# Handing the row maxima of an attention step to the score banks through memory instead of through TensorE

## The chip, the cores and the metric

The kernel runs on one core of one Trainium2 chip. The metric is the device time of one execution in microseconds (us). All times below are either such whole times or come from one profiled execution of the kernel before the change.

## What is computed

Two transformer-like layers with a residual stream of 4 x 1024 tokens of 128 values. The change touches only the attention of layer 0:

```
qkv = X @ W_qkv                      # 16 heads of 64, batch 4, 1024 tokens
scores = einsum("bqhd,bkhd->bhqk", q, k) / scale
weights = softmax(scores)            # over the keys
attn = einsum("bhqk,bkhd->bqhd", weights, v)
s = attn @ W_out
x = x + s * silu(mixture_of_experts(xn))
```

The rest (the router and the experts of layer 0, a recurrence and a 4-bit feed-forward part in layer 1) runs before and behind it and is not changed.

## The kernel before, in words

`layer0_attention` handles N = 32 pairs of heads (4 batches x 8 pairs), in a hardware loop whose body is two pairs. A pair `n` has 16 steps `t`. Steps 0 to 7 are the first half of the queries (512 of them), steps 8 to 15 the second; each step is one tile of 128 keys against 512 queries for both heads, so a score tile is 128 x 1024. Two steps make a visit `p = t // 2`; `VISIT[p]` lists small extra items that TensorE does in that visit: projections `K0`, `K1`, `Q0`, `Q1` of a later pair, `V0`, `V1`, the denominators `den0`, `den1`, the output projections `out0`, `out1`. All items write one bank, `ps_x`, so an item waits until the item before it in the list has been read (`bank_free`).

The softmax needs a bound of each query's scores before the exponential. That bound is the row maximum over a cheaper score product: in every step `row_max` on TensorE writes the tile `ps_m` (queries as rows, one bank pair, so it waits for the reduction of the one before: semaphore `m_done`), and VectorE reduces it into `mxh`. Eight of these make a unit (one half of the queries of one pair), and then one small reduction collects them. Units run `EARLY` steps ahead of the scores that need them.

Scores are accumulated on top of the negated maximum. There are two score banks, `ps_s[0]` and `ps_s[1]`, used by even and odd steps. Before TensorE may accumulate (`scores`, six matmuls, waits for `seeded`), the bank must hold the negated maximum, the same in all 128 rows. In the kernel before this is done in four stages: TensorE transposes the maxima with the identity (items `max0` and `max1`, L1241, into `ps_x`); VectorE multiplies them with a mask into `shift` (L1560); TensorE multiplies `shift` with ones into `ps_s[0]` (`spread`, L1293, once before each half, waits for the exponential that last read the bank); ScalarE copies that bank to a tile in SBUF, `shift_all` (`keep_shift`, L1444), and from there into the banks of the other seven steps (`seed`, L1449).

ScalarE then takes the exponential from the score bank into a ring of 8 probability tiles (L1464), GpSimd adds these up for the denominators (L1529), TensorE multiplies them with V three steps late (`values`, L1301). SyncE moves V, the batch's normalised inputs and a part of the experts' weights between memory and SBUF; it issues its DMAs from one queue in program order, and each wait there holds back all that stand behind it. The order of work on every engine is written out by hand in the loop bodies.

## Time and profile before

| what | before |
|---|---|
| median of 3 runs (lowest to highest) | 1915.51 us (1915.51 to 1917.42) |
| the profiled execution's own time | 1918.03 us |
| its span in the trace | 1916.2 us |
| mean granted TensorE clock | 0.982 of full speed |

The attention loop fills about three quarters of the span. Because its body repeats, one pair read closely in the middle of the run tells what all 32 cost; times are read as start and duration within the span.

### The profile page before, as it was taken

How to read it: one execution, taken by the hardware profiler on the slowest of the kernel's cores; microseconds unless marked ns; L12 is line 12 of the kernel's file. 1: busy time of each engine (PE TensorE's matmuls, PEld its weight loads, DVE VectorE, ACT ScalarE, POOL GpSimd, SP SyncE). 2: the span in 40 equal slices, each digit the busy share in tenths (PEclk: the TensorE clock that was granted, in tenths of full speed). 3: DMA queues.
4: the chain of work that ended last, by engine and by line, in shares of the span. 5: the costliest groups of instructions: out<-in, count | busy, mean ns of one | idle time of the engine just before them, and what ended most of it. 6: DMA issues, size and time to landing. Idle time of an engine off the chain costs nothing. (4 is left out here: it accounts for less than half of the span.)

```text
span 1916.2 us, 32241 instructions
## 1 busy us (share of the span) xinstructions
PE 1776.4 (93%) x9630; PEld 958.1 (50%) x9630; DVE 1486.4 (78%) x2052; ACT 1485.6 (78%) x2017; POOL 1434.9 (75%) x870
## 2 busy tenths in 40 slices
PE   5799999999999999999999999999999899985688
PEld 4444444444444444444444444444444488863456
DVE  6777777777777777777777777777777698888896
ACT  4488888888888888888888888888888688874553
POOL 4388888888888888888888888888888456765663
PEclk9999999999999999999999999999999999997898
DMA  7101010101011010101010101011010477531000
GB/s 248 46 13 55 11 56 15 59 11 55 22 44 42 25 55 11 55 11 55 12 55 19 55 20 46 22 44 56 11 55 11 153 230 247 158 99 50 1 17 28
DMA packets 98438, 108.95 MB, mean 57 GB/s; under 512 B 8161, under 2 KB 88097, under 8 KB 95202
## 3 DMA queue, kind: packets, MB, share of 16 engines
q1 hardware_dynamic: 93410, 98.26, 16.1%
q0 software_dynamic: 4992, 10.27, 1.6%
q8 instruction: 16, 0.26, 0.1%
q14 instruction: 20, 0.16, 0.0%
HBM read 53.12 MB, written 27.38 MB: 42 GB/s over the span
## 5 line engine op out<-in xcount | busy, mean ns | idle before, releaser
L1529 POOL TENSOR_TENSOR psum_k<-psum_k,probs 128x1024 f32<-128x1024 f32 x384 | 926.4, 2412 | 183.7 <-ACT probs L1464 168.6
L1546 DVE TENSOR_REDUCE mxh<-ps_m 128x2 f32<-128x1024 f32 x518 | 628.4, 1213 | 276.1 <-PE ps_m L1273 275.7
L1464 ACT ACTIVATE probs<-ps_s 128x1024 f32<-128x1024 f32 x512 | 496.4, 1022 | 132.4 <-PE ps_s L1286 93.2
L1301 PE MATMUL ps_v<-probs,V 128*64 128x512 f32 x2056 | 489.8, 597 | 0.0
L1449 ACT ACTIVATE ps_s<-qkv_raw 128x1024 f32<-128x1024 f32 x449 | 445.9, 1030 | 7.1
L1570 DVE RECIPROCAL e_y_row<-e_y_row 128x128 f32<-128x128 f32 x256 | 241.8, 945 | 30.2 <-ACT e_y_row L1420 21.1
L1301 PEld LDWEIGHTS ps_v<-probs,V 128*64 128x64 f32 x2056 | 137.6, 137 | 224.9 <-issue 188.4
L1529 POOL TENSOR_TENSOR psum_k<-probs 128x1024 f32<-128x1024 f32 x64 | 152.4, 2381 | 65.7 <-ACT probs L1464 57.9
L1286 PE MATMUL ps_s<-e_ew 64*128 64x512 f32 x1536 | 198.9, 390 | 1.1 <-ACT qkv_raw L1444 1.0
L1286 PEld LDWEIGHTS ps_s<-e_ew 64*128 64x128 f32 x1536 | 145.9, 184 | 28.6 <-ACT qkv_raw L1444 1.4
L859 POOL DMA_INDIRECT results<-e_y_row,e_y_at x92 | 103.7, 1128 | 67.4 <-ACT e_y_row L800 45.2
L1273 PE MATMUL ps_m<-e_ew 64*128 64x512 f32 x524 | 131.5, 498 | 11.4 <-DVE mxh L1546 10.2
L1273 PE MATMUL ps_m<-k_hi,q_hi 64*128 64x512 f32 x512 | 128.0, 496 | 4.0 <-DVE mxh L1546 3.6
L1273 PEld LDWEIGHTS ps_m<-e_ew 64*128 64x128 f32 x524 | 49.1, 184 | 114.8 <-DVE mxh L1546 68.2
L1286 PE MATMUL ps_s<-q_hi,k_lo 64*128 64x512 f32 x512 | 101.6, 391 | 0.0
L1286 PE MATMUL ps_s<-q_hi,k_hi 64*128 64x512 f32 x512 | 101.5, 391 | 0.0
L1286 PE MATMUL ps_s<-q_lo,k_hi 64*128 64x512 f32 x512 | 101.2, 389 | 0.0
L1273 PEld LDWEIGHTS ps_m<-k_hi,q_hi 64*128 64x128 f32 x512 | 47.6, 183 | 106.5 <-DVE mxh L1546 60.1
L784 ACT ACTIVATE e_relu<-e_ps_z 128x512 f32<-128x512 f32 x124 | 74.2, 598 | 26.5 <-PE e_ps_z L713 25.6
L905 DVE TENSOR_TENSOR e_h_lo<-e_relu,e_h_hi 128x512 fp32r<-128x512 f32 x124 | 87.5, 711 | 1.2 <-ACT e_h_hi L789 1.2
L901 DVE TENSOR_TENSOR e_relu<-e_relu 128x512 f32<-128x512 f32 x108 | 74.5, 690 | 15.5 <-ACT e_relu L784 15.2
L789 ACT ACTIVATE e_h_hi<-e_relu 128x512 fp32r<-128x512 f32 x124 | 78.2, 631 | 6.0 <-DVE e_relu L901 5.9
(322 smaller groups left out, 2938.1 us busy)
## 6 DMA issues: line engine op xcount, KB each, us to landing
e_ew<-w_split SPq DMA_DIRECT2D x23, 1024.0 KB
V<-e_x_raw SPq DMA_DIRECT2D x33, 512.0 KB, 3.6
xs_hi<-xh SPq DMA_DIRECT2D x16, 512.0 KB, 4.1
xs_lo<-xl SPq DMA_DIRECT2D x16, 512.0 KB, 4.7
rows<-in_blank_d SPq DMA_DIRECT2D x4, 1483.5 KB, 16.2
e_x_raw<-rows SPq DMA_DIRECT2D x23, 258.0 KB, 3.0
we_raw<-in_experts_d SPq DMA_DIRECT2D x33, 128.0 KB, 2.5
w_split<-we_hi SPq DMA_DIRECT2D x32, 128.0 KB, 1.9
```

The costliest lines, as they stand in the source:

```text
L789: nc.scalar.activation(h_hi[:, q % NH, :], r2[:, q % NH, :], ACT.Copy).then_inc(hi_done, 1)
L859: nc.gpsimd.indirect_dma_start(g.results[:, :], bass.IndirectOffsetOnAxis(ap=y_at[s][:, t, 0:1], axis=0), y_row[s][:, t, :], None).then_in ...
L901: nc.vector.tensor_tensor(r2[:, q % NH, :], r[:, q % NZ, :], r[:, q % NZ, :], ALU.mult).then_inc(sq_done, 1)
L905: nc.vector.tensor_tensor(h_lo[:, q % NH, :], r2[:, q % NH, :], h_hi[:, q % NH, :].bitcast(F32), ALU.subtract).then_inc(lo_done, 1)
L1273: ins = nc.tensor.matmul(m[:, x, :], q_hi[par][rows, q:q + P], k_hi[par][rows, kh * CH:(kh + 1) * CH], start=True, stop=True)
L1286: ins = nc.tensor.matmul(o[:, x, :], lhs[par][rows, keys], rhs[par][rows, qs], start=False, stop=True, skip_group_check=True)
L1301: ins = nc.tensor.matmul(ps_v[rows, :], V[par][:, kt, rows], probs[:, t % RING, x, :], start=kt == 0, stop=kt == KT - 1)
L1449: nc.scalar.activation(ps_s[t % 2][:, :, :], shift_all[:, :, :], ACT.Copy).then_inc(seeded, 1)
L1464: nc.scalar.activation(probs[:, t % RING, :, :], ps_s[t % 2][:, :, :], ACT.Exp, scale=SCALE).then_inc(p_done, 1)
L1529: nc.gpsimd.tensor_tensor(acc, probs[:, (t - 1) % RING, :, :] if kt == 1 else acc, probs[:, t % RING, :, :], ALU.add).then_inc(add_done, 1)
L1546: nc.vector.tensor_reduce(mxh[:, kh, t, :], max_bank(unit, i)[:, :, :], AX.X, ALU.max).then_inc(m_done, 1)
L1570: ins = nc.vector.reciprocal(rden[:, cols], den[:, cols])
```

## The change

The maxima no longer pass through TensorE and VectorE. The small reduction writes them to `mx` (128 x 2 x 4). SyncE stores them to a buffer of 4 KB in memory, `g.peaks`, in an order that turns them into rows (1024 separate elements of 4 bytes), waits for that transfer, and loads the row broadcast to all 128 partitions of `peak[hf]` (512 KB). ScalarE copies `peak`, times -1, into the score banks in all 16 steps. `EARLY` goes from 3 to 4. The items are spread anew over the visits, with at most one of them between the scores and `values`; `K0` is made one pair earlier, in the last visit; ScalarE reads the first item of a visit before it seeds the banks, and the second one after it.

The constants and the tables of items:

```diff
-    EARLY = 3
+    EARLY = 4
-    VISIT = [("out0", "K0"), ("den1", "Q0"), ("max1", "V0"), ("K1",), ("out1",), ("den0", "Q1"), ("max0", "V1"), ()]
-    LATE = ("K1", "out1")
+    VISIT = [("out0",), ("Q0", "den1"), ("V0",), ("K1",), ("Q1", "den0"), ("V1",), ("out1",), ("K0",)]
-    FIRST = ["K0", "Q0", "K1", "Q1", "V0", "V1", "V2", "max0", "V3"]
+    FIRST = ["K0", "Q0", "K1", "Q1", "V0", "V1", "V2", "V3", "K0+"]
```

On SyncE:

```diff
+            def spread(unit, hf):
+                sp.wait_ge(mx_done, unit + 1)
+                sp.dma_start(g.peaks[hf:hf + 1, :].rearrange("a (x t q) -> q (a x) t", x=2, t=4), mx[:, :, :],
+                             allow_slow_non_contiguous=True).then_inc(mx_out, 16)
+                sp.wait_ge(mx_out, unit * 16 + 16)
+                sp.dma_start(peak[hf][:, :, :].rearrange("p x c -> p (x c)"), g.peaks[hf:hf + 1, :].to_broadcast([P, 2 * CH])).then_inc(peak_in, 16)
...
+                spread(n * 2 + 1, 1)
                 expert_part(n)
                 load_part(n + 1)
+                spread(n * 2 + 2, 0)
+                spread(n * 2 + 3, 1)
                 expert_part(n + 1)
                 load_part((n + 2) % N)
+                spread(n * 2 + 4, 0)
```

On TensorE:

```diff
-            def max_rows(n, name):
-                bank_free(n, name)
-                pe.wait_ge(mx_done, 1 if n is None else n * 2 + (2 if name == "max1" else 3))
-                for x, rows in enumerate(HEADS):
-                    ins = nc.tensor.matmul(bank(n, name)[rows, 0:P], mxw[:, x, :], g.ident[:, :], start=True, stop=True)
-                ins.then_inc(x_ready, 1)
...
-                    if t % KT == KT - 1:
-                        pe.wait_ge(shift_done, n * 2 + t // KT + 2)
-                        pe.wait_ge(p_done, P0 + n * STEPS + t)
-                        spread(1 - t // KT, 0).then_inc(spread_ready, 1)
                     for name in VISIT[p][:1]:
-                        if name not in LATE:
-                            item(n, par, name, b)
+                        item(n, par, name, b)
```

On ScalarE:

```diff
-            def keep_shift(k):
-                act.wait_ge(spread_ready, k)
-                nc.scalar.activation(shift_all[:, :, :], ps_s[0][:, :, :], ACT.Copy).then_inc(seeded, 1)
+            def seed(n, t):
+                hf = t // KT % 2
+                if t % KT < 2:
+                    act.wait_ge(peak_in, peaks_of(n, t))
+                act.wait_ge(p_done, P0 + n * STEPS + t - 1)
+                nc.scalar.activation(ps_s[t % 2][:, :, :], peak[hf][:, :, :], ACT.Copy, scale=-1.0).then_inc(seeded, 1)
...
                     for name in VISIT[p][:1]:
-                        if name[:3] != "den":
-                            read(n, name, 1 - par)
+                        read(n, name, par if name == "K0" else 1 - par)
+                    for k in (t + 1, t + 2):
+                        seed(n, k)
                     if p == 0:
                         keep_values(n * 2 + 1)
+                        expert_part(n)
```

On VectorE one operation goes:

```diff
-            def shifts(n, name):
-                hf = int(name[3])
-                v.wait_ge(x_ready, nth(n, name))
-                nc.vector.tensor_tensor(shift[hf][:, :].rearrange("p (j q) -> p j q", j=4),
-                                        bank(n, name)[:, 0:P].unsqueeze(1).to_broadcast([P, 4, P]),
-                                        mask[:, :].unsqueeze(2).to_broadcast([P, 4, P]), ALU.mult).then_inc(shift_done, 1)
```

On VectorE the order behind the reductions of the 16 steps becomes: `out0` added after 1; `Q0` and the experts' part after 3; parts of the reciprocal after 4, 5, 6 and 8; `K1` after 7; `Q1` and the normalising product after 9; reciprocal after 10, 11, 12 and 14; `out1` added after 13; `K0` and the second normalising product after 15.

Three places of the program show how the instructions move. The first is TensorE in the visit of steps 4 and 5 and the one behind it, before: `ps_m` is the row maximum's tile, `mxw` the collected maxima, `V0` the values of this pair.

```order
L1273 MATMUL ps_m<-k_hi1,q_hi1 128x512 [waits m_done]
L1273 MATMUL ps_m<-k_hi1,q_hi1 128x512
L1201 REGISTER_ALU
L1241 MATMUL ps_x<-ident,mxw 64x128 [waits mx_done,xv_done]
L1241 MATMUL ps_x<-ident,mxw 64x128
L1301 MATMUL ps_v<-probs,V0 64x512 [waits p_done]
...
L1273 MATMUL ps_m<-k_hi1,q_hi1 128x512 [waits m_done]
L1273 MATMUL ps_m<-k_hi1,q_hi1 128x512
L1373 REGISTER_ALU [waits shift_done]
L1293 MATMUL ps_s0<-shift0,ones_r 128x512 [waits p_done]
L1293 MATMUL ps_s0<-shift0,ones_r 128x512
```

The transposition of the maxima stands ahead of the values, and one visit or two later the spreading matmuls stand there, each behind a wait; in the changed kernel neither line exists, and the row maximum is followed by at most one item and then by the values.

The second place is ScalarE behind the exponential of step 7, where the second half of the queries begins. Before:

```order
L1464 ACTIVATE probs<-ps_s1 128x1024 [waits add_done]
L1443 REGISTER_ALU
L1444 ACTIVATE qkv_raw<-ps_s0 128x1024 [waits spread_ready]
L1472 REGISTER_ALU
L1448 REGISTER_ALU [waits seeded]
L1449 ACTIVATE ps_s1<-qkv_raw 128x1024 [waits p_done]
L1410 REGISTER_ALU
L1412 ACTIVATE k_hi1<-ps_x 128x512 [waits x_ready]
```

And in the changed kernel:

```order
L1463 ACTIVATE probs<-ps_s1 128x1024 [waits add_done]
L1408 REGISTER_ALU
L1410 ACTIVATE k_hi1<-ps_x 128x512 [waits x_ready]
L1445 REGISTER_ALU
L1446 REGISTER_ALU [waits peak_in]
L1447 ACTIVATE ps_s0<-peak1 128x1024 [waits p_done]
L1446 REGISTER_ALU [waits peak_in]
L1447 ACTIVATE ps_s1<-peak1 128x1024 [waits p_done]
```

The copy out of the bank has become a copy into it, the count of ScalarE's large instructions is the same (two for these two banks), the reading of the item stands ahead of them, and the wait is now for a DMA.

The third place is SyncE's queue in the first pair of the loop body, where only DMAs and their waits matter. Before:

```order
L1149 DMA V<-e_x_raw 128x8x128 [waits v_ready]
...
L1170 DMA xs_hi<-xh 128x1024
...
L1171 DMA xs_lo<-xl 128x1024
...
L1155 DMA w_split<-we_hi 128x256
```

And in the changed kernel:

```order
L1147 DMA V<-e_x_raw 128x8x128 [waits v_ready]
...
L1177 DMA xs_hi<-xh 128x1024
...
L1178 DMA xs_lo<-xl 128x1024
...
L1163 DMA peaks<-mx 128x8x1 [waits mx_done]
...
L1166 DMA peak<-peaks 128x1024 [waits mx_out]
...
L1153 DMA w_split<-we_hi 128x256
```

The store and the broadcast load stand behind the three large loads of every second pair and ahead of the stores of the experts' part.

## Rows read from the trace of the kernel before

**Rows 1.** The windows view of one pair: length, busy time by engine, granted clock.

```profile
745.97:790.72 44.75, 43.53 (x247) 20.86 (x245) 34.03 (x38) 37.31 (x46) 36.98 (x21) 1.00 0.05 17
```

**Rows 2.** One line's instructions (once per pair): duration, first and last start.

```profile
L1402 ACT ACTIVATE wo<-wout_raw x32: 292/294/298, 121.5 to 1509.5; 128x128 f32 x32
```

**Rows 3.** Timeline of TensorE: start, duration, what, idle time before it.

```profile
755.62 0.50 PE L1273 MATMUL ps_m<-k_hi,q_hi 64*128 64x512 f32 x2
756.30 1.08 PE L1250 MATMUL ps_x<-psum_k,ones 128*64 128x512 f32 x4 [0.17 <-DVE e_ew L1554]
757.20 1.89 PE L1301 MATMUL ps_v<-probs,V 128*64 128x512 f32 x8
...
761.74 0.50 PE L1273 MATMUL ps_m<-e_ew 64*128 64x512 f32 x2
762.56 0.44 PE L1241 MATMUL ps_x<-ident,mxw 128*64 128x128 f32 x4 [0.32 <-DVE e_ew L1554]
762.83 1.89 PE L1301 MATMUL ps_v<-probs,V 128*64 128x512 f32 x8
...
767.37 0.50 PE L1273 MATMUL ps_m<-e_ew 64*128 64x512 f32 x2
767.94 0.49 PE L1293 MATMUL ps_s<-shift,ones_r 64*128 64x512 f32 x2
768.37 1.94 PE L1301 MATMUL ps_v<-probs,V 128*64 128x512 f32 x8
...
771.13 0.50 PE L1273 MATMUL ps_m<-e_ew 64*128 64x512 f32 x2
...
772.95 0.49 PE L1273 MATMUL ps_m<-e_ew 64*128 64x512 f32 x2
773.37 1.94 PE L1301 MATMUL ps_v<-probs,V 128*64 128x512 f32 x8
...
776.10 0.50 PE L1273 MATMUL ps_m<-e_ew 64*128 64x512 f32 x2
...
778.21 0.50 PE L1273 MATMUL ps_m<-e_ew 64*128 64x512 f32 x2 [0.22 <-DVE mxh L1546]
```

**Rows 4.** Timeline of ScalarE over one visit.

```profile
755.12 1.94 ACT L1464 ACTIVATE probs<-ps_s 128x1024 f32<-128x1024 f32 x2 [0.61 <-PE ps_s L1286]
757.42 0.60 ACT L1420 ACTIVATE e_y_row<-ps_x 128x512 f32<-128x512 f32 x1 [0.36 <-PE ps_x L1250]
757.91 1.97 ACT L1449 ACTIVATE ps_s<-qkv_raw 128x1024 f32<-128x1024 f32 x2
```

**Rows 5.** Timeline of VectorE: reduction, collecting, subtraction, reciprocal.

```profile
760.46 1.22 DVE L1546 TENSOR_REDUCE mxh<-ps_m 128x2 f32<-128x1024 f32 x1 [1.46 <-PE ps_m L1273]
761.72 0.17 DVE L1549 TENSOR_REDUCE mxw<-mxh 128x8 f32<-128x16 f32 x1
761.81 0.69 DVE L1554 TENSOR_TENSOR e_ew<-ps_x,e_ew 128x512 fp32r<-128x512 f32 x1
...
764.37 0.95 DVE L1570 RECIPROCAL e_y_row<-e_y_row 128x128 f32<-128x128 f32 x1
```

**Rows 6.** DMA issues: how many, KB each, median us from issue to landing.

```profile
V<-e_x_raw SPq DMA_DIRECT2D x33, 512.0 KB, 3.6
...
xs_lo<-xl SPq DMA_DIRECT2D x16, 512.0 KB, 4.7
...
we_raw<-in_experts_d SPq DMA_DIRECT2D x33, 128.0 KB, 2.5
w_split<-we_hi SPq DMA_DIRECT2D x32, 128.0 KB, 1.9
```

**Rows 7.** The DMA view of 878 to 883 us, when one move of V runs alone.

```profile
DMA packets 1040, 0.52 MB, mean 105 GB/s; under 512 B 16, under 2 KB 1040, under 8 KB 1040
```

**Rows 8.** Timelines at the start of the attention: the first maximum, the first scores.

```profile
68.12 0.17 DVE L1549 TENSOR_REDUCE mxw<-mxh 128x8 f32<-128x16 f32 x1
...
76.32 0.96 PE L1286 MATMUL ps_s<-e_ew 64*128 64x512 f32 x6 [0.97 <-ACT qkv_raw L1444]
```

More of the change, by code:

```diff
@@ L1010, in layer0_attention @@
     k_hi, k_lo, q_hi, q_lo = ([even[k], sb(f"{name}1", [P, T], F32R)] for k, name in enumerate(("k_hi", "k_lo", "q_hi", "q_lo")))
-    shift = [sb(f"shift{h}", [P, CH], F32R) for h in range(2)]
-    shift_all = qkv[:, 2, :, :].rearrange("p a d -> p (a d)").rearrange("p (x c) -> p x c", c=CH)
+    peak = [qkv[:, 2, :, :].rearrange("p a d -> p (a d)").rearrange("p (x c) -> p x c", c=CH), sb("peak1", [P, 2, CH], F32)]
     V_next = g.V_next
@@ L1057, in layer0_attention @@
     mx_done = sem("mx_done")
[L1058 removed]
+    mx_out = sem("mx_out")
+    peak_in = sem("peak_in")
     x_ready = sem("x_ready")
@@ L1257, in out_projection @@
                 pe.wait_ge(attn_done, n * 2 + (2 if hf else 1))
+                if not hf:
+                    pe.wait_ge(wo_staged, n + 1)
                 for rows in HEADS:
@@ L1288, in scores @@
                 ins.then_inc(s_ready, 1)
-            def spread(hf, k):
-                for x, rows in enumerate(HEADS):
-                    ins = nc.tensor.matmul(ps_s[k][:, x, :], ones_r[rows, :], shift[hf][rows, :], start=True, stop=True)
-                return ins
             def values(n, par, t, seen):
@@ L1339, in _ @@
             first_max(0, 4, 5, 6, 7)
-            first("V0", "V1", "V2", "max0")
+            first("V0", "V1", "V2", "V3")
             pe.wait_ge(hi_done, rounded(None, "Q1"))
             first_max(1, *range(EARLY))
-            first("V3")
+            pe.wait_ge(n_read, 1)
+            pe.wait_ge(m_done, KT + EARLY)
+            for k in range(2):
+                for x, rows in enumerate(HEADS):
+                    ins = nc.tensor.matmul(ps_s[k][:, x, :], k_hi[0][rows, 0:P], q_hi[0][rows, 0:CH], start=True, stop=True)
+            ins.then_inc(armed, 1)
+            first("K0+")
             pe.wait_ge(preset, LATE_PRESETS)
+            pe.wait_ge(xa_done, AHEAD["a"])
             pe.wait_ge(xv_done, AHEAD["v"])
-            pe.wait_ge(n_read, 1)
             for x, rows in enumerate(HEADS):
                 nc.tensor.matmul(ps_v[rows, :], ones[:, :], probs[:, 0, x, :], start=True, stop=False)
-            pe.wait_ge(shift_done, 1)
-            pe.wait_ge(m_done, KT + EARLY - 1)
-            spread(0, 1)
-            spread(0, 0).then_inc(spread_ready, 1)
             for n, par in pairs(pe):
-                b = (n + 1) // PAIRS % B
                 for t in range(STEPS):
                     p = t // 2
+                    b = (n + (2 if p == VISITS - 1 else 1)) // PAIRS % B
                     unit, i = maximum(t)
@@ L1388, in _ @@
                         values(n, par, t - 2, False)
-                    for name in VISIT[p]:
-                        if name in LATE or name != VISIT[p][0]:
-                            item(n, par, name, b)
+                    for name in VISIT[p][1:]:
+                        item(n, par, name, b)
             item(N, 0, LAST[0], 0)
@@ L1406, in read @@
             def read(n, name, par):
-                if name[:3] in ("max", "out"):
+                if name[:3] == "out":
                     return
@@ L1419, in read @@
                 else:
+                    act.wait_ge(rden_done, n * 2 + (2 if name == "den0" else 1))
                     nc.scalar.activation(den[:, :], ps_x[:, :], ACT.Copy).then_inc(xa_done, 1)
@@ L1548, in row_max @@
                     v.wait_ge(m_done, unit * KT + KT)
-                    nc.vector.tensor_reduce(mxw[:, :, 0:4], mxh[:, :, :, :].rearrange("p k t x -> p x t k"), AX.X, ALU.max).then_inc(mx_done, 1)
+                    if not (isinstance(unit, int) and unit == 0):
+                        v.wait_ge(mx_out, unit * 16)
+                    nc.vector.tensor_reduce(mx[:, :, :], mxh[:, :, :, :].rearrange("p k t x -> p x t k"), AX.X, ALU.max).then_inc(mx_done, 1)
             def low(n, name, par):
@@ L1690, in _ @@
                 step(2)
-                low(n, "K0", nxt)
                 step(3)
+                low(n, "Q0", nxt)
+                expert_part(n)
+                step(4)
                 inverse(n, 1, 0)
-                step(4)
-                low(n, "Q0", nxt)
                 step(5)
-                shifts(n, "max1")
                 inverse(n, 1, 1)
@@ L2450, in layouts @@
     blank[:, D] = 2 * NT + np.arange(ROUTED * CH)
-    mask = np.zeros((2, DH, 4), np.float32)
-    for j in range(4):
-        mask[:, j, j] = -1.0
     return {
@@ L2467, in layouts @@
         "wout_d": c(a["L0_attn_W_out"].reshape(PAIRS, P, D).transpose(1, 0, 2)),
-        "mask_d": c(mask.reshape(P, 4)),
         "place_d": c(np.arange(2 * NT, dtype=np.uint32).reshape(2, TILES, P).transpose(2, 0, 1)),
```

118 lines of the change are left out of this document (54 added, 64 removed).

## The prediction

> **What bounds the kernel now.** I read the busy times of one pair first. In a pair of 44.75 us TensorE is busy 43.53, ScalarE 37.31, GpSimd 36.98 and VectorE 34.03, at a granted clock of 1.00 [rows 1]. That this pair is typical follows from a line that runs once per pair: its 32 executions start from 121.5 to 1509.5 us, so a pair takes 1388.0 / 31 = 44.77 us, and 32 pairs take 1433 us [rows 2]. TensorE paces the loop; the other three have 7 to 11 us of room per pair. Then I read TensorE's timeline of that pair for what it does and where it waits.
>
> The plain case is a visit with one item: from one row maximum of an even step (771.13) to the next (776.10) it takes 4.97 us [rows 3]. The reader should see three distances there. From a row maximum of an odd step (772.95) to what follows (773.37) it is 0.42 to 0.43 us. A denominator item starts at 756.30 and the values at 757.20, so an item costs 0.90. Anything beyond these distances is a wait.
>
> **What is removed on TensorE.** The transposition of the maxima: the row maximum starts at 761.74, the item at 762.56 (0.82 later, of which 0.43 are the row maximum and the rest a wait for VectorE's subtraction on the shared bank), and the values at 762.83, so the item itself takes 0.27. Together 0.82 - 0.43 + 0.27 = 0.66 us, twice per pair: 1.32. The spreading: 767.37 to 768.37 is 1.00 us where 0.43 would do, so 0.57, twice per pair: 1.14. The re-spread items remove two more waits: the denominator item that stood behind `K0`'s subtraction on the same bank (755.62 to 756.30 is 0.68 where 0.43 would do: 0.25), and a row maximum held up by a late VectorE at 778.21; 1.82 behind 776.10, as from 771.13 to 772.95, would be 777.92, so 0.29. All four are in [rows 3]. Sum of the removals: 1.32 + 1.14 + 0.25 + 0.29 = 3.0 us a pair.
>
> The same from the other side: the changed list has six visits with one item and two with two (`Q0` with `den1`, `Q1` with `den0`). 6 x 4.97 + 2 x (4.97 + 0.90) = 41.6 us, which is 3.2 below 44.77. I take 3.1. Over 32 pairs that is 99 us.
>
> **Whether ScalarE can follow.** It keeps 16 large copies and 16 exponentials per pair; two copies change direction, and I take a copy times -1 for as long as a copy without (0 more; a single look at both kinds would be needed to say otherwise; if each of 16 cost 0.1 us more it would be 1.6 us of ScalarE's room of 7). What changes is the order inside a visit. Let S be the start of the scores of the even step: it lies a third of a us behind that step's row maximum, and the odd step's row maximum follows at S + 1.48 (771.13 to 772.95 is 1.82), so S is 754.14 in the visit whose odd row maximum starts at 755.62 [rows 3]. The visit's rhythm on ScalarE [rows 4]: two exponentials from 755.12, about S + 1.0, the next operation 1.82 later at the earliest; a read takes 0.49 to the next start, two seeds 1.97. In the changed visit TensorE's item ends at about S + 2.9, the read starts there, the seeds at S + 3.4, the first bank is ready at S + 4.4 and the second at S + 5.4. TensorE wants the first at S + 4.97 and the second 0.7 later at S + 5.67. So the slack is 0.5 us and 0.3 us. It holds, but it is the tightest place on an engine, and the exponentials of the next visit start at S + 6.0, only 0.6 behind the seeds. Moving the read ahead of the seeds is costed at nothing because of those 0.3 us; without them each visit with such a read (six) would pay the difference.
>
> VectorE loses the mask product twice a pair. Its worst visit is the last: reciprocal, reduction to about S + 3.5, subtraction of `K0` and normalising product, together about 1.5 us by rows of 0.69 and 1.22 and 0.95 [rows 5], ends at S + 5.0, and the next reduction is wanted at S + 5.2. Hidden by 0.2 us. GpSimd's work is the same 37 us in a pair of 41.6.
>
> **Whether the two transfers arrive in time.** This is the wait that the change adds. The unit for the second half is collected by VectorE 3.4 us behind the scores of step 2; the bank that needs it is seeded 3.4 us into the visit of steps 6 and 7, which is 5.87 + 4.97 us later: 10.8 us of time. For the first half of the next pair a reciprocal stands before the reduction, which ends at S + 3.7; two plain visits and 3.4 us give 9.6 us of time.
>
> The chain is: wake SyncE, store, wake SyncE, load, wake ScalarE. For the wakes I take 0.5 us in all, an estimate. No row shows a store of 1024 elements of 4 bytes or a load that reads one row of 4 KB 128 times. For the store the lower bound is the store of 128 rows, 1.9 us, and the upper one the move of V, 3.6 us [rows 6], which is the same number of pieces (1040 packets, [rows 7]) of 512 bytes each. I take 2.6, nearer to the short one, as the pieces are small. For the load the lower bound is the 128 KB load of 2.5 us and the upper one the third of three queued 512 KB loads, 4.7 us; I take 3.5. The chain is then 0.5 + 2.6 + 3.5 = 6.6 us, and 8.8 us with both upper bounds. Both fit into 9.6. Behind the SyncE queue's wait for the store stand the load, the experts' stores and the move of V, which have a visit or more of room. In every second pair three 512 KB transfers are issued some 3.5 us before the first store; they have landed within 6 us, so they can add up to about 2.5 us to a chain with 10.8 us of time. Hidden too.
>
> The Trainium skill, page "DMA: Bandwidth & Descriptors", speaks against this store in two places: its "Specifications" say that below 512 B the DMA engines do a read-modify-write, and its "Rules for kernel authors" say that a strided last dimension lowers to one descriptor per element. The count of pieces agrees with how V's move shows in the trace; what a read-modify-write costs for 4 bytes in memory no run shows yet.
>
> **Before and behind the loop.** Before the loop a fourth early maximum (1.1 us), the copy, product and subtraction of the second `K0` (0.9 + 0.6 + 0.7) come onto the path, the mask product and one matmul pass go (about -0.7 and -0.4): together +3 us with the arming of the banks. The first transfer starts when the first unit is collected at 68.3 us and would land at 75, before the first scores at 76.3 [rows 8], so it adds nothing.
>
> **Sum.** 1918.0 (the profiled execution's own time, span 1916.2) - 99 + 3 = 1822. The runs' median is 2.5 us below that execution, so 1819.5 in terms of the median; I say 1819. Its own range is 1806 (41.3 a pair) to 1835 (0.5 us of small waits per pair).
>
> **Rivals.**
> - *The change as costed*, TensorE paces, 1806 to 1835: 0.54.
> - *ScalarE's new order sets the pace.* For it: slack of 0.3 us before the second bank, in six visits. Against it: 4.4 us from exponential to exponential is less than 4.97. If each visit pays 0.25 to 0.35 us, 2.0 to 2.8 us a pair come back: 1885 to 1905; half of that 1850. Chance 0.17, mostly 1835 to 1885.
> - *The chain is a little too long*, between 9.6 and 11.8 us, above my upper bounds. Each us beyond 9.6 costs one us a pair, and beyond 10.8 two: at 10.6 us it is 32 us, 1851. Chance 0.15.
> - *Slower than before: the 4-byte store.* If the pieces go one by one with a round trip each, the store grows with the 64 pieces that each of 16 engines has. The gain of 3.1 is used up when (L - 9.6) + (L - 10.8) = 3.1, at a chain of L = 11.8 us. With the load at 3.5 and 0.5 of wakes that is a store of 7.8 us, or (7.8 - 1.9) / 64 = 92 ns per piece over the short store. V's move, (3.6 - 1.9) / 64 = 27 ns per piece, speaks against it, but it ends in SBUF and not in memory. At 150 ns a piece the store takes 11.5, L is 15.5, the pair pays 10.6 - 3.1 = 7.5 us: 1819 + 10.6 x 32 = 2158; at 100 ns L is 12.3, 4.2 us come in, 1953. It is the rule on read-modify-write of the page named above that would do this. Chance 0.12.
> - *No change within 0.2%*: gains and such waits cancel: 0.02.
>
> **How the numbers follow.** A measurement of this kernel tells a change from none at about 0.2%, 4 us. Faster: 0.54 + 0.17 + 0.15 = 0.86; same 0.02; slower 0.12. The predicted time is that of the first case, 1819. The range leaves out the slower case (0.12), the few above 1880 and those below 1806 (0.05), so 1806 to 1880; the likeliest case alone has 1806 to 1835.
>
> **What would show it.** The once-per-pair line should start every 41.6 us. TensorE's distance from a row maximum to the values or the item behind it should be 0.43 everywhere. ScalarE's first two seeds of a half should show no wait for a DMA; if they do, the DMA view gives the store's time to landing, which I have at 2.6 us, and the load's, at 3.5. If ScalarE sets the pace, scores wait for seeds in all visits alike, and not only at the start of a half. What would make me wrong is above all a store that lands after 6 us or more, or a broadcast that is served slowly because all 128 rows come from one place in memory.

## The result, and the profile after

The changed kernel takes 2198.98 us (median of 4 runs, 2195.74 to 2202.12) against 1916.47 us before on the same chip: a ratio of 1.147 (95% interval 1.145 to 1.149). It is slower by 282 us, where 1819 us and faster had been forecast.

The page's line on the whole and on the engines, of the changed kernel: busy time, share of the span, instructions.

```profile
span 2198.2 us, 31591 instructions
...
PE 1860.1 (85%) x9247; PEld 995.3 (45%) x9247; DVE 1445.8 (66%) x1989; ACT 1494.6 (68%) x2018; POOL 1440.2 (66%) x868
```

No engine has become the bound: the busiest, TensorE, has 15% of the span idle. So something that is no engine's work is waited for. The once-per-pair line (as [rows 2]) and the windows view of one pair (as [rows 1]) size it. A second windows line is from the variant that stores the maxima as 512 pieces of 8 bytes (below), in which nothing is late:

```profile
L1397 ACT ACTIVATE wo<-wout_raw x32: 292/293/293, 138.5 to 1799.5; 128x128 f32 x32
```

```profile
883.90:937.50 53.60, 46.16 (x234) 21.99 (x234) 33.12 (x35) 37.47 (x46) 37.15 (x20) 0.91 0.15 39
```

```profile
880.00:922.10 42.10, 41.95 (x236) 19.65 (x234) 33.50 (x36) 38.55 (x46) 37.31 (x21) 1.00 0.16 50
```

A pair takes (1799.5 - 138.5) / 31 = 53.58 us where it took 44.77: 8.81 more. Over the 31 pairs between these starts that is 273 us; the first of the starts comes 17 us later than before (121.5), with the first waits for a transfer ahead of it, and what lies behind the last one is 8 us shorter (398.7 us, before 406.7). Together that is the 282 us. ScalarE, VectorE and GpSimd do nearly what they did. TensorE is busy 46.16 us with fewer matmuls (x234, before x247), at a granted clock of 0.91. Beside the variant with 8-byte pieces, which has the same work, it is idle 7.44 us instead of 0.15 and busy 4.2 us longer: these two, 7.3 and 4.2 us, make up the 11.5 us between the two pairs.

What is waited for stands in the view of waits: who waits, for what, us in total, times, longest.

```profile
ACT ps_s L1447 <- DMA qkv_raw<-peaks: 142.9, 32, 5.7
ACT ps_s L1447 <- DMA peak<-peaks: 129.1, 32, 5.1
```

```profile
SPq L1166 <- DMA peaks<-mx: 590.8, 62, 10.9
```

ScalarE's first seed of each half waits for the broadcast load (which the trace names `peak` in one half and, by the place it lies in, `qkv_raw` in the other), 272 us in all. In front of the load SyncE's queue stands for 590.8 us behind the store, 590.8 / 62 = 9.5 us each time. One place, from SyncE's timeline and the DMA issues (the last column is the median from issue to landing, us):

```profile
919.36 0.39 SPq L1163 DMA_DIRECT2D peaks<-mx  x1
...
930.07 0.32 SPq L1166 DMA_DIRECT2D qkv_raw<-peaks  x1
```

```profile
qkv_raw<-peaks SPq DMA_DIRECT2D x33, 512.0 KB, 4.2
...
peak<-peaks SPq DMA_DIRECT2D x32, 512.0 KB, 4.5
```

The store is issued at 919.36, the load only at 930.07, 10.7 us later; the load itself then takes 4.2 to 4.5. The DMA view of 919 to 931 us shows that the store's packets are not what takes the time. Its row is the busy share of the 16 DMA engines in 40 slices of 0.3 us, in tenths:

```profile
DMA  0000473000000000000000000000000000000000
...
DMA packets 1040, 0.00 MB, mean 0 GB/s; under 512 B 1040, under 2 KB 1040, under 8 KB 1040
```

All 1040 packets have been through the engines within two us of the issue, in about one us of work (slices 5 to 7); the other 9 us are spent behind them, before the transfer is reported as done. ScalarE and TensorE at the half that waits for this load (start, duration, what, idle before it):

```profile
928.64 0.60 ACT L1410 ACTIVATE k_hi<-ps_x 128x512 fp32r<-128x512 f32 x1
...
934.50 1.97 ACT L1447 ACTIVATE ps_s<-qkv_raw 128x1024 f32<-128x1024 f32 x2 [5.26 <-DMA qkv_raw<-peaks]
```

```profile
930.41 0.50 PE L1280 MATMUL ps_m<-e_ew 64*128 64x512 f32 x2
...
935.58 2.83 PE L1293 MATMUL ps_s<-e_ew 64*128 64x512 f32 x12 [4.68 <-ACT ps_s L1447]
```

ScalarE is idle 5.26 us, TensorE 4.68, and the twelve score matmuls that follow take 2.83 us. In the variant without transfers (below) the same twelve take 1.55. The windows view gives the granted clock: 0.56 from 935.58 to 936.80, 0.50 from there to 938.20, and 1.00 again from 940.00. So TensorE comes out of the idle stretch at its lower clock level and is back at full speed within some 4 us. Two shorter waits of the same run, 3.64 us before 961.71 and 3.32 before 1282.44, are followed by twelve matmuls in 2.30 and 2.20 us.

### The profile page after: what moved, and what is told of

Same layout as the page of the kernel before. It is cut to its first block and busy times, and to the rows that moved or that the text cites. A ratio compares the mean times of both kernels' runs of the same rounds, so it can differ in the third digit from the quotient of the medians.

```text
span 2198.2 us, 31591 instructions
## 1 busy us (share of the span) xinstructions
PE 1860.1 (85%) x9247; PEld 995.3 (45%) x9247; DVE 1445.8 (66%) x1989; ACT 1494.6 (68%) x2018; POOL 1440.2 (66%) x868
## 5 line engine op out<-in xcount | busy, mean ns | idle before, releaser
L1302 PE MATMUL ps_v<-probs,V 128*64 128x512 f32 x2056 | 507.6, 615 | 0.0
L1447 ACT ACTIVATE ps_s<-qkv_raw 128x1024 f32<-128x1024 f32 x256 | 252.0, 1021 | 142.9 <-DMA qkv_raw<-peaks 142.9
L1293 PE MATMUL ps_s<-e_ew 64*128 64x512 f32 x1536 | 237.7, 447 | 126.7 <-ACT ps_s L1447 124.4
L1447 ACT ACTIVATE ps_s<-peak 128x1024 f32<-128x1024 f32 x256 | 252.3, 1024 | 129.1 <-DMA peak<-peaks 129.1
L1293 PEld LDWEIGHTS ps_s<-e_ew 64*128 64x128 f32 x1536 | 160.7, 211 | 171.3 <-ACT ps_s L1447 138.2
L1293 PE MATMUL ps_s<-q_hi,k_hi 64*128 64x512 f32 x512 | 120.4, 465 | 105.4 <-ACT ps_s L1447 105.4
L1293 PE MATMUL ps_s<-q_lo,k_hi 64*128 64x512 f32 x512 | 116.1, 446 | 0.0
L1293 PE MATMUL ps_s<-q_hi,k_lo 64*128 64x512 f32 x512 | 115.8, 446 | 0.0
L1293 PEld LDWEIGHTS ps_s<-q_hi,k_hi 64*128 64x128 f32 x512 | 55.6, 213 | 123.3 <-ACT ps_s L1447 116.5
L1266 PE MATMUL ps_x<-e_y_row,wo 128*64 128x512 f32 x260 | 91.8, 793 | 0.8 <-issue 0.8
```

The source lines that it names most:

```text
L1266: ins = nc.tensor.matmul(ps_x[rows, :], wo[1 - par][:, rows], attn[:, :], start=True, stop=True)
L1293: ins = nc.tensor.matmul(o[:, x, :], lhs[par][rows, keys], rhs[par][rows, qs], start=False, stop=True, skip_group_check=True)
L1302: ins = nc.tensor.matmul(ps_v[rows, :], V[par][:, kt, rows], probs[:, t % RING, x, :], start=kt == 0, stop=kt == KT - 1)
L1447: nc.scalar.activation(ps_s[t % 2][:, :, :], peak[hf][:, :, :], ACT.Copy, scale=-1.0).then_inc(seeded, 1)
```

## The experiments

Where did 10 us of store come from, and does the rest of the change hold? *Theory A*: each small piece costs a round trip, so the count of pieces sets the time (the slower rival as it was written). *Rival B*: the broadcast load, or the DMAs queued around it, are what is late. *Rival C*: it isn't the store alone, the new order of work costs time too. *Theory D*, called that of shared stretches in the later expectations: the place of the pieces in memory sets the time, many small ones side by side. Each ratio is to the kernel before, timed beside the variant on the same chip: 1917.31 us there for the first three variants, 1928.44 for the next three, 1917.32 for the last.

**The store as 128 pieces of 32 bytes.** Each partition writes its eight maxima side by side; ScalarE puts them in order as it reads, over a stride of 32 bytes.

```diff
-                sp.dma_start(g.peaks[hf:hf + 1, :].rearrange("a (x t q) -> q (a x) t", x=2, t=4), mx[:, :, :],
-                             allow_slow_non_contiguous=True).then_inc(mx_out, 16)
+                sp.dma_start(g.peaks[hf:hf + 1, :].rearrange("a (q k) -> (a q) k", k=8), mx[:, :, :].rearrange("p x t -> p (x t)")).then_inc(mx_out, 16)
...
+                return row[:, :, :].rearrange("p a c -> p (a c)").rearrange("p (q x t) -> p x t q", x=2, t=4)
```

> The store of the maxima keeps its 4 KB and its place, but goes as 128 pieces of 32 bytes (one per partition) instead of 1024 of 4; the order is put right by ScalarE, which reads the loaded row with a stride of 32 bytes when it seeds the banks. Result unchanged. Theory A (the store costs by its number of pieces in memory: the changed kernel waits 10.7 us for 1024 pieces where 128 rows of 1 KB take 1.9, so 8.6 ns a piece): store 2 to 3 us, chain 7 to 8 us, no wait of ScalarE for the load, a pair of about 41.6 us, 1815 to 1835 us. Rival B (the broadcast load, or the DMAs queued around it, are what is late): the store's form changes little, 2100 us or more. Rival C (the new order of the engines' work is slow by itself): slower than 1916 us even with a short store. A strided read on ScalarE that costs more than a plain one would show as seeds over 1.02 us and would add 16 times the excess to each pair's work on ScalarE, from about 0.25 us each also to the time.

2236.03 us, ratio 1.166 (1.164 to 1.168). SyncE's timeline, then the groups by line (busy, mean ns of one, idle before it):

```profile
912.26 0.32 SPq L1163 DMA_DIRECT2D peaks<-mx  x1
...
913.66 0.32 SPq L1165 DMA_DIRECT2D peak<-peaks  x1
```

```profile
L1452 ACT ACTIVATE ps_s<-peak 128x1024 f32<-128x1024 f32 x256 | 526.3, 2104 | 0.0
```

The same group in the changed kernel:

```profile
L1447 ACT ACTIVATE ps_s<-peak 128x1024 f32<-128x1024 f32 x256 | 252.3, 1024 | 129.1 <-DMA peak<-peaks 129.1
```

The store is done in 1.4 us, and no seed waits for a DMA (0.0 where it was 129.1). But a strided seed takes 2.10 us instead of 1.02. That is (2.104 - 1.024) x 16 = 17.3 us more a pair; 37.5 + 17.3 = 54.8 is close to the pair that this run has, 54.6, of which ScalarE is busy 52.7 (880.00 to 934.60). ScalarE sets the pace. The time of 1815 to 1835 us in the expectation was missed for that reason, which it had named, and the whole time says nothing on the chain; the store's own time does. It also speaks against Rival B: the load and the DMAs around it are as before, and nothing is late. The Trainium skill, page "SBUF — State Buffer", section "Specifications (TRN2)", gives 16-byte lines, with at least two hits in a line needed for full bandwidth. By that a stride of 32 bytes is slow and one of 8 is free. The first half of this agrees with 2.10 against 1.02.

**No transfers at all.** Both transfers and their waits are left out, and the exponential is taken of the scores times 1e-6, so that nothing overflows; the maxima are computed and not used.

```diff
-            def spread(unit, hf):
...
-                if t % KT < 2:
-                    act.wait_ge(peak_in, peaks_of(n, t))
...
-                    nc.scalar.activation(probs[:, t % RING, :, :], ps_s[t % 2][:, :, :], ACT.Exp, scale=SCALE).then_inc(p_done, 1)
+                    nc.scalar.activation(probs[:, t % RING, :, :], ps_s[t % 2][:, :, :], ACT.Exp, scale=1e-6).then_inc(p_done, 1)
```

> Both transfers are left out (the banks are seeded from tiles that nothing refreshes, and the exponential's scale is set to 1e-6 so that all stays finite; the output is therefore not the attention's). All other instructions and their order are those of the changed kernel. Theory A and rival B: no wait is left, about 41.6 us a pair, 1815 to 1835 us. Rival C: the new order is the loss, over 1900 us. Between (1840 to 1900): small waits of the new order, which would then be read from this run.

1832.46 us, ratio 0.957 (0.955 to 0.959). The once-per-pair line, and TensorE's timeline at a half's first scores:

```profile
L1383 ACT ACTIVATE wo<-wout_raw x32: 297/300/304, 123.5 to 1426.6; 128x128 f32 x32
```

```profile
921.92 1.55 PE L1279 MATMUL ps_s<-e_ew 64*128 64x512 f32 x12
```

A pair takes (1426.6 - 123.5) / 31 = 42.04 us, where the prediction had 41.6. Rival C falls: the new order of work, ScalarE's included, brings nearly all that was costed, and the whole loss of 53.58 - 42.04 = 11.5 us a pair comes with the transfers.

**512 pieces of 8 bytes.** The two heads' maxima of a query lie side by side in `mx` and in memory; ScalarE reads `peak` over a stride of 8 bytes. Everything else is as in the changed kernel.

```diff
-    g.mx = sb("mx", [P, 2, 4], F32)
+    g.mx = sb("mx", [P, 4, 2], F32)
...
-                sp.dma_start(g.peaks[hf:hf + 1, :].rearrange("a (x t q) -> q (a x) t", x=2, t=4), mx[:, :, :],
+                sp.dma_start(g.peaks[hf:hf + 1, :].rearrange("a (g q r) -> q (a g) r", q=P, r=2), mx[:, :, :].rearrange("p (g s) x -> p g (s x)", s=1),
...
+                return nc.scalar.activation(bank[:, :, :], row[:, :, :].rearrange("p a c -> p (a c)").rearrange("p (c x) -> p x c", x=2),
+                                            ACT.Copy, scale=-1.0)
...
-                    nc.vector.tensor_reduce(mx[:, :, :], mxh[:, :, :, :].rearrange("p k t x -> p x t k"), AX.X, ALU.max).then_inc(mx_done, 1)
+                    nc.vector.tensor_reduce(mx[:, :, :], mxh[:, :, :, :].rearrange("p k t x -> p t x k"), AX.X, ALU.max).then_inc(mx_done, 1)
```

> As the changed kernel, but the store goes as 512 pieces of 8 bytes, and ScalarE reads the row with a stride of 8 bytes. Result unchanged. Theory A, by 8.6 ns a piece: store 1.9 + 4.4 = 6.3 us, chain 0.5 + 6.3 + 4.3 = 11.1 us against 9.6 and 10.8 us of room, so 1.5 + 0.3 = 1.8 us of waits a pair, 1819 + 58 = about 1877 us, with 1850 to 1930 for the clock. If the bytes or one fixed round trip to memory set the store's time and not the pieces, it stays near 2190 us.

1834.41 us, ratio 0.957 (0.956 to 0.959). The once-per-pair line; SyncE's timeline; the seeds:

```profile
L1397 ACT ACTIVATE wo<-wout_raw x32: 292/310/326, 124.2 to 1428.8; 128x128 f32 x32
```

```profile
911.96 0.39 SPq L1163 DMA_DIRECT2D peaks<-mx  x1
...
916.18 0.32 SPq L1166 DMA_DIRECT2D qkv_raw<-peaks  x1
...
932.13 0.38 SPq L1163 DMA_DIRECT2D peaks<-mx  x1
...
937.60 0.33 SPq L1166 DMA_DIRECT2D peak<-peaks  x1
```

```profile
L1442 ACT ACTIVATE ps_s<-peak 128x1024 f32<-128x1024 f32 x256 | 277.0, 1126 | 0.0
```

The pair is (1428.8 - 124.2) / 31 = 42.08 us, within 0.04 of the one without transfers. From the store's issue to the load's it is 4.2 us, and 5.5 behind the three large loads. Half the pieces, and less than half the time: Theory A had expected 6.3 us of store and 1877 us in all, and both were missed, on the good side. The seed costs 0.10 us more (1.126 against 1.024), 16 x 0.10 = 1.6 us a pair, hidden in ScalarE's room. By the section of the Trainium skill named above, "SBUF — State Buffer", "Specifications (TRN2)", this stride is free; the measured 10% decides.

**The store by itself.** A kernel that does nothing but such stores and loads, six of each, one at a time.

```diff
+                    go(same4.rearrange("a (x t q) -> q (a x) t", x=2, t=4), mx[:, :].rearrange("p (x t) -> p x t", x=2))
...
+                    go(half4.rearrange("a (t q) -> q a t", t=4), mx[:, 0:4].rearrange("p (x t) -> p x t", x=1))
...
+                    go(quarter4.rearrange("a (t q) -> q a t", t=2), mx[:, 0:2].rearrange("p (x t) -> p x t", x=1))
...
+                    go(rows32, mx[:, :])
...
+                    go(strided(apart4, 8, 128, 1), mx[:, :].unsqueeze(2))
...
+                    go(strided(mid32, 8, 16, 8), big[:, :, 0:8])
...
+                    go(to4[:, :, 0:1], mx[:, :].unsqueeze(2))
...
+                    go(bc[:, :], same4.to_broadcast([P, 1024]))
...
+                    go(bw[:, :], wide)
```

> No attention at all: SyncE issues single DMAs one after the other, each six times and each waited for, and the output is zeros. Theory A: 1024 pieces of 4 bytes into one 4 KB piece of memory take about 10.7 us from issue to the next issue, 512 about 6.3, 256 about 4.1, 128 of 32 bytes 2 to 3; the same 1024 pieces into SBUF take under 3.6. What is open, and what this tells apart: whether it is the small size (1024 pieces of 32 and 64 bytes would be as slow, 1024 of 512 bytes fast, about 4 to 5 us), the closeness of pieces of different engines in one place of memory (then 1024 pieces of 4 bytes that lie 512 bytes apart would be fast), or only the count of writes into memory (then all with 1024 pieces take about 10). The broadcast load from one 4 KB row: 3.5 to 4.3 us, and the same 512 KB from 128 different rows the same if the one row is no bottleneck.

DMA issues; the names begin with `m_` for memory and `s_` for SBUF, and the number is that of pieces. `m_1024x` is the changed kernel's store, `m_apart` the same 1024 pieces of 4 bytes 512 bytes from one another, `m_1024x<-big` 1024 pieces of 32 bytes that begin 64 bytes from one another, `s_1024x` 1024 pieces of 4 bytes into SBUF (eight in each partition, 8 bytes from one another, so not side by side), `b_mem` the broadcast of one row of 4 KB, `b_wide` the same bytes from 128 rows of their own.

```profile
b_mem<-m_1024x SPq DMA_DIRECT2D x6, 512.0 KB, 3.6
b_wide<-m_wide SPq DMA_DIRECT2D x6, 512.0 KB, 3.5
...
m_1024x<-big SPq DMA_DIRECT2D x6, 32.0 KB, 2.4
m_128x<-mx SPq DMA_DIRECT2D x7, 4.0 KB, 1.4
m_1024x<-mx SPq DMA_DIRECT2D x6, 4.0 KB, 9.7
...
m_256x<-mx SPq DMA_DIRECT2D x6, 1.0 KB, 9.2
m_apart<-mx SPq DMA_DIRECT2D x6, 4.0 KB, 2.8
s_1024x<-mx SPq DMA_DIRECT2D x6, 4.0 KB, 2.3
```

Theory A falls here: a quarter of the pieces takes as long (9.2 against 9.7), and all 1024 take 2.8 when they lie apart. Theory D stands. A size under 512 bytes isn't enough to be slow either: 1024 pieces of 4 and of 32 bytes, lying apart, take 2.8 and 2.4 us, and 1024 of 512 bytes take 3.5. That the store into SBUF is short (2.3) can't be put down to SBUF, as its pieces do not lie side by side; no run writes such pieces densely into SBUF. The broadcast is no slower than a plain load, so Rival B falls as well, and with it the second fear of the prediction.

**256 pieces of 16 bytes, with nothing strided on ScalarE.** Row maximum `t` takes every fourth query instead of 128 in a row, so that each partition's four maxima of a head are neighbours. The stride moves to TensorE's weight load. The computation is the same.

```diff
-                sp.dma_start(g.peaks[hf:hf + 1, :].rearrange("a (x t q) -> q (a x) t", x=2, t=4), mx[:, :, :],
-                             allow_slow_non_contiguous=True).then_inc(mx_out, 16)
+                sp.dma_start(g.peaks[hf:hf + 1, :].rearrange("a (x q t) -> q (a x) t", x=2, t=4), mx[:, :, :]).then_inc(mx_out, 16)
...
-                    ins = nc.tensor.matmul(m[:, x, :], q_hi[par][rows, q:q + P], k_hi[par][rows, kh * CH:(kh + 1) * CH],
+                    every4 = q_hi[par][rows, hf * CH:(hf + 1) * CH].rearrange("d (q t) -> d q t", t=4)[:, :, t]
+                    ins = nc.tensor.matmul(m[:, x, :], every4, k_hi[par][rows, kh * CH:(kh + 1) * CH],
```

> As the changed kernel, but the row maximum of tile t takes every fourth query instead of 128 neighbouring ones, so that the four maxima of a partition lie side by side: the store goes as 256 pieces of 16 bytes, ScalarE reads plainly. Result unchanged. The theory on the store is now: not the count but how many pieces fall into the same short stretch of memory sets its time (1024, 512 and 256 dense pieces of 4 bytes took 9.7, 9.3 and 9.2 us, the same 1024 lying 512 bytes apart 2.8, and 8-byte pieces 4.2 in the loop). Four 16-byte pieces share 64 bytes here where the changed kernel has 16 of 4 bytes and the run with 8-byte pieces 8: store about 3 us, no wait, 42.0 us a pair, 1825 to 1840 us, at or a little below the run with 8-byte pieces (1834) as its seeds cost 1.02 and not 1.13 us. Rival: only pieces of 4 bytes are slow and the sharing is chance: the same time here. What could spoil it: TensorE loading weights with a stride of 16 bytes; if that costs 0.1 us a row maximum, 16 of them add 1.6 us a pair, 1885 us.

1899.33 us beside 1928.44 before, ratio 0.985 (0.984 to 0.987).

```profile
L1279 PE MATMUL ps_m<-k_hi,q_hi 64*128 64x512 f32 x512 | 159.5, 619 | 0.0
```

```profile
peaks<-mx SPq DMA_DIRECT2D x65, 4.0 KB, 2.5
```

The store lands in 2.5 us, near the 3 expected, and no seed waits for its load. But a row maximum takes 0.62 us where the kernel without transfers has 0.50, and the load of its weights 305 ns instead of 183. So the expected 1825 to 1840 us were missed, by what the expectation had named as able to spoil it. 16 x 0.12 = 1.9 us a pair on the engine that sets the pace, and the pair is 43.75, 1.7 above 42.04. The stride costs about as much an instruction as the one of 8 bytes on ScalarE (0.10), but that engine had room for it.

**The 1024 pieces, but 64 bytes apart.** They go into another buffer; the load reads zeros (and the exponential is of the scores times 1e-6), so the maxima are not used, but both transfers and all waits are there.

```diff
-                sp.dma_start(g.peaks[hf:hf + 1, :].rearrange("a (x t q) -> q (a x) t", x=2, t=4), mx[:, :, :],
+                sp.dma_start(g.apart[hf:hf + 1, :].rearrange("a (k q s) -> q (a k) s", k=8, s=16)[:, :, 0:1], mx[:, :, :].rearrange("p x t -> p (x t)").unsqueeze(2),
```

> As the changed kernel with 1024 pieces of 4 bytes, but each piece goes to a place 64 bytes from the next, in another buffer, and the load, still behind the wait for the store, reads a buffer of zeros (the maxima are not used, and the exponential's scale is 1e-6 so that all stays finite). Theory of shared stretches: store 2.5 to 3 us, no wait for the load, about 1835 us. Theory of the number of pieces or of their size of 4 bytes: store near 10.7, about 2190 us.

1847.23 us beside 1928.44 before, ratio 0.958 (0.957 to 0.960).

```profile
apart<-mx SPq DMA_DIRECT2D x65, 4.0 KB, 2.6
```

```profile
L1400 ACT ACTIVATE wo<-wout_raw x32: 297/299/302, 125.3 to 1428.7; 128x128 f32 x32
```

This is the run that isolates the cause inside the kernel: same count, same size, same queue, same waits. The store lands in 2.6 us, the pair takes (1428.7 - 125.3) / 31 = 42.05, and the whole loss is gone. One thing more differs, that the load does not read what was just stored; the single stores above, which wait for no load, show the same difference (9.7 and 2.8 us).

**The dense store, and nobody waits for it.** It goes into a buffer of its own; the load is issued right behind it, without the wait, and reads zeros (exponential as above).

```diff
-                sp.dma_start(g.peaks[hf:hf + 1, :].rearrange("a (x t q) -> q (a x) t", x=2, t=4), mx[:, :, :],
+                sp.dma_start(g.aside[hf:hf + 1, :].rearrange("a (x t q) -> q (a x) t", x=2, t=4), mx[:, :, :],
...
-                sp.wait_ge(mx_out, unit * 16 + 16)
```

> The dense store of 1024 pieces of 4 bytes is kept as it is, but into a buffer of its own, and SyncE issues the load at once, which reads a buffer of zeros (maxima not used, exponential's scale 1e-6). Only the wait between the two is gone. If the loss is the latency that stands in the chain: about 1835 us, with the store still taking 9 us or more to land. If the store slows the DMA engines or the other transfers while it is under way: the loads land late and the time is over 1900 us.

2111.04 us beside 1928.44 before, ratio 1.093 (1.089 to 1.097).

```profile
qkv_raw<-peaks SPq DMA_DIRECT2D x33, 512.0 KB, 12.9
...
V<-e_x_raw SPq DMA_DIRECT2D x33, 512.0 KB, 13.5
...
w_split<-we_hi SPq DMA_DIRECT2D x32, 128.0 KB, 12.0
```

```profile
ACT ps_s L1450 <- DMA qkv_raw<-peaks: 113.3, 32, 4.4
```

Of the two cases of the expectation the second came: the store is not only late, it delays others. The load behind it lands after 12.9 us, V's move after 13.5 and the experts' store after 12.0, where the kernel with the pieces 64 bytes apart has 3.8, 5.1 and 3.2. A pair takes 50.55 us, and ScalarE's seeds wait for the load although nobody waits for the store. These transfers depend on the store in nothing. Nor is it only the report of their end that comes late: in the DMA view of 923 to 939 us (store issued at 923.86, load at 924.28) the load's data moves mostly at 10 to 20 GB/s from 928.2 to 934.6, and at 195 to 358 GB/s from 935.4 on. The Trainium skill, page "DMA: Bandwidth & Descriptors", section "Back-pressure in remote DMA", says "Stalled writes stall the source SDMA engine's other queues too." It says so of writes between cores and of other queues. Here the writes go to memory and the transfers that wait stand in the same queue; whether another queue would have been spared, no run shows.

**How close is close.** Single stores of 1024 pieces, at several distances and sizes.

```diff
+                for name, step in steps.items():
+                    times(spread[name].rearrange("k (q s) -> q k s", s=step)[:, :, 0:1], row8)
...
+                times(own[:, 0:8].unsqueeze(2), wide8[:, :, 0:1])
+                times(runs8.rearrange("k (q s) -> q k s", s=2), mx[:, :].rearrange("p (k s) -> p k s", s=2))
...
+                times(one_row.rearrange("k q -> q k").unsqueeze(2), mx[:, 0:1].unsqueeze(2))
```

> No attention; output zeros; single stores into memory, each six times and waited for. 128 partitions x 8 pieces of 4 bytes, neighbouring partitions 4, 8, 16, 32, 64 and 256 bytes apart. Theory of shared stretches with a stretch of 64 bytes and about 0.5 us for each piece that shares one: 9.5, 5.5, 3.5, 2.7, 2.5, 2.5 us to landing; with a stretch of 32 bytes (one DMA engine's share of eight partitions) the same up to 16 bytes, and 2.5 from 32 on. Pieces of 8, 16 and 32 bytes laid densely: about 5, 3 and 1.5 to 2 us. If only different engines' writes collide: 8 pieces of one partition side by side are fast (2.5); if any two writes to one stretch collide they take 5. Only 32 or 64 of the partitions, dense: as 128 (about 9.5), as the stretches are as full. One piece per partition, one dense row of 512 bytes: 9 us too, though it has an eighth of the pieces.

`every_four` has the neighbours every 4 bytes (dense), and so on; `own_adjacent` has the eight pieces of one partition side by side, `one_line_row` is one dense row of 128 pieces.

```profile
every_four<-mx SPq DMA_DIRECT2D x6, 4.0 KB, 10.0
every_eight<-mx SPq DMA_DIRECT2D x6, 4.0 KB, 4.2
every_sixteen<-mx SPq DMA_DIRECT2D x6, 4.0 KB, 3.0
...
every_sixtyfour<-mx SPq DMA_DIRECT2D x6, 4.0 KB, 2.5
...
own_adjacent<-mx_strided SPq DMA_DIRECT2D x6, 4.0 KB, 5.4
...
one_line_row<-mx SPq DMA_DIRECT2D x6, 0.5 KB, 8.2
```

The time falls with the distance, to that of free pieces at 16 to 64 bytes. One row of 128 pieces already takes 8.2 of the 10.0; seven more rows add 1.8. Dense pieces of 8, 16 and 32 bytes took 3.6, 2.3 and 1.4 us. Neighbours need not come from different partitions: `own_adjacent` takes 5.4, twice the time of free pieces. One forecast failed: the dense rows filled by the first 64 or the first 32 partitions alone were to take as long as with 128, but took 8.9 and 4.9 us. How full a short stretch is can't be all that counts.

**Which pieces collide.** Stores of few pieces. Two readings: those in one stretch of 256 bytes are served one by one, or those in a stretch of 64.

```diff
+                row("sixtyfour_in_a_row", 64, 1, 1)
+                row("thirtytwo_in_a_row", 32, 1, 1)
+                row("sixteen_in_a_row", 16, 1, 1)
+                row("sixteen_in_eight_rows", 16, 1, 8)
...
+                row("sixtyfour_every_eight", 64, 2, 1)
+                row("sixtyfour_every_sixteen", 64, 4, 1)
...
+                row("sixtyfour_in_eight_rows", 64, 1, 8)
```

> No attention; output zeros; single stores of 4-byte pieces from the first 16, 32, 64 or 128 partitions, neighbouring partitions side by side unless the name says otherwise, in one row or in eight rows 4 KB apart, each six times and waited for. Two readings of the earlier probe. One: pieces that fall into the same 256 bytes are served one after the other, about 0.13 us each (64 such pieces: 8.2 us; 32: 4.2 and 4.9; 16: 3.0; under that a floor of 2.5). Then: 64 in a row 8.2 us though there are only 64 pieces, 32 in a row 4.2, 16 in a row 2, 16 in eight rows 2.5, 32 every eight bytes 4.2, 64 every eight bytes 4.2, 64 every sixteen 2.5 to 3, 128 in a row 8.2, 64 in eight rows 9. Two: 64 bytes filled by 16 pieces are what is slow: then 64, 32 and 16 in a row and 16 in eight rows all take 8 us or more, and every eight bytes 4.2 whatever the count.

```profile
sixtyfour_in_a_row<-mx SPq DMA_DIRECT2D x6, 0.2 KB, 7.1
thirtytwo_in_a_row<-mx SPq DMA_DIRECT2D x6, 0.1 KB, 4.9
sixteen_in_a_row<-mx SPq DMA_DIRECT2D x6, 0.1 KB, 2.5
sixteen_in_eight_rows<-mx SPq DMA_DIRECT2D x6, 0.5 KB, 5.1
...
sixtyfour_every_eight<-mx SPq DMA_DIRECT2D x6, 0.2 KB, 3.9
sixtyfour_every_sixteen<-mx SPq DMA_DIRECT2D x6, 0.2 KB, 1.7
```

64, 32 and 16 pieces in a row take 7.1, 4.9 and 2.5 us, and 128 took 8.0. It is not a full stretch of 64 bytes that costs (16 in a row fill one, and are cheap); the single rows fit the reading of 256 bytes roughly (8.2, 4.2 and 2 had been forecast). But 16 in each of eight rows took 5.1 us, where that reading had 2.5, and 64 in each of eight rows, 4 KB apart, took 20.7, where it had 9. No reading of mine gives this. The exact law stays open.

**The version with 8-byte pieces, again.** The kernel of the third experiment, unchanged.

> The kernel with 512 pieces of 8 bytes once more, in more rounds, as the version that beats both: ratio to before 0.957, between 0.955 and 0.959, as in the run before.

1834.94 us (1833.44 to 1837.38), ratio 0.957 (0.956 to 0.958): 82 us below the kernel before, timed beside it, and 364 below the changed one.

## Why the prediction was wrong, point by point

- **The bound and the removals: right.** 41.6 us a pair and 3.1 us gained were forecast; without transfers it is 42.04 and 2.7, and with 8-byte pieces 42.08. The whole gain with 8-byte pieces is 4.3%, 82 us, where 99 were costed in the loop and 3 given back around it.
- **ScalarE's new order: right.** Its slack of 0.3 us holds, even with seeds that are 0.10 us dearer. That rival (0.17) is not seen anywhere; where ScalarE does set the pace, with the stride of 32 bytes, it is by dearer seeds and not by the order. A copy times -1 costs no more than a plain one, as assumed: 1.02 us, before 1.03.
- **Before and behind the loop: near.** +3 us were forecast. Without transfers the first once-per-pair line comes 2.0 us later than before (123.5 against 121.5) and the part behind the last one is 3.1 us shorter. But that the first transfer adds nothing was wrong with the slow store: it was to land at 75 us, its load was issued only at 78.68, and the first seed began at 82.89.
- **The load: a little low.** 3.5 us taken, 4.2 to 4.5 measured, below the upper bound of 4.7; alone it would have cost nothing.
- **The store: this step failed.** The term was "I take 2.6, nearer to the short one, as the pieces are small", with 3.6 as its upper bound; from its issue to that of the load it measured 10.7. The count of pieces was compared with V's move, and the size was taken to make it only shorter. Neither decides: small pieces that lie close together in memory are slow, and V's move has nothing of the kind, as its pieces are of 512 bytes and end in SBUF. With the pieces 64 bytes apart the term is 2.6 us, just as taken, and the loss is gone. The row was the nearest by count and the farthest by what mattered.
- **The room of the chain: about right; a term for the clock is missing.** With 10.7 and 4.2 to 4.5, and the 0.5 estimated for wakes but in part inside the 10.7, L is about 15.2 (from the store's issue at 919.36 to the seed at 934.50 it is 15.1). Then (15.2 - 9.6) + (15.2 - 10.8) = 10.0 us of waits a pair. Measured are 272 / 32 = 8.5 us of ScalarE's waits, and 7.3 us of TensorE's idle time. What the sum leaves out is the lower clock behind each stall: TensorE is busy 4.2 us a pair longer. So 42.0 + 10.0 = 52.0 comes near to the measured 53.58 by two errors that partly cancel. Why the waits are shorter than 10.0 no run took apart; that the slower visits give the chain more time is my guess.
- **The rival that came true, with another mechanism.** "At 150 ns a piece the store takes 11.5, L is 15.5 ... 2158" was near the measured 2199. But its law was false, so the nearness is luck: pieces do not cost 150 ns each, since 256 take about as long as 1024 and 1024 apart take 2.6. Nor is the size alone to blame, to which the prediction tied this case by the read-modify-write: pieces of 4 and 32 bytes that lie apart are cheap. Whether a read-modify-write is at work in the dense store no run shows. Had one halved the pieces by dropping half of them, it would have gained next to nothing. It got 0.12, because the upper bound was set by V's move; a bound from a row that lacks the feature in question is no bound, and the range should have reached to this case.

## What to carry to other kernels

A transfer into memory of 128 to 1024 single 4-byte elements side by side, from 128 partitions, takes 8 to 10 us here; pairs of elements (8 bytes) bring it to about 4, and so does a distance of 8 bytes between single ones. Where a layout must be turned on the way, put the stride where it is cheapest: here a read over 8 bytes on an engine with room (0.10 us an instruction), not a read over 32 bytes (1.08) and not the weight load of the engine that sets the pace (0.12, all of it lost). When no row of the trace shows a transfer of the kind that is to be added, measure it alone before it is put on a chain with 10 us of room.

## What the runs showed of the hardware

- Stores into memory of 4-byte pieces side by side, from 128 partitions: 8 to 10 us for 128 to 1024 pieces; with a piece every 8 bytes 4.2 us, every 64 bytes 2.5. From fewer partitions a single row takes less (64 pieces 7.1, 16 pieces 2.5), but 64 in each of eight rows 4 KB apart take 20.7. In the store that was looked at, the packets were through the DMA engines after some 2 us of 10.7.
- Transfers queued behind such a store land only after it: 12.9 us instead of 3.8, 13.5 instead of 5.1.
- One row of 4 KB broadcast to 128 partitions loads as fast as 128 rows: 3.6 and 3.5 us.
- ScalarE, 128 x 1024 of 4 bytes: 1.02 us dense, 1.13 over a stride of 8 bytes, 2.10 over 32. TensorE's row maximum: 0.50 us, and 0.62 with weights over a stride of 16 bytes (the load of the weights 305 ns instead of 183).
- Behind a stall of 4.7 us TensorE's granted clock is 0.50 to 0.56 for the next twelve matmuls, which take 2.83 us instead of 1.55; behind stalls of 3.3 and 3.6 us they take 2.20 and 2.30.
